# Small full-precision products packed into single passes, and the setup spread over the first steps, in a four-block convolution and attention kernel

## The chip, the cores and the metric

The kernel runs on one core of a Trainium2 chip. The metric is the device time of one execution in microseconds, the median of several. A core has the engines TensorE (PE, with its weight loads as PEld), VectorE (DVE), ScalarE (ACT), GpSimd (POOL) and SyncE (SP), which issues most DMAs. Each runs its own list of instructions in order and waits on semaphores for the others.

## What is computed

The input `x` is 32 images of 256 channels by 28 x 28 positions. Four blocks follow one another, each `x = x + block(gn(x))`, where `gn` is a group norm over 32 groups. Shortened, with the weights' names cut:

```python
# block 0: gated mix of 8 experts, one 256x256 matrix per image
g = sparsemax(gn_x.mean(axis=(2, 3)) @ gate_w.T + gate_b)
out = einsum('boi,bihw->bohw', einsum('bk,koi->boi', g, expert_w), gn_x)
# block 1: 3x3 depthwise, batch norm, relu, prune, 1x1, batch norm, relu, prune
h = prune(relu(bn(depthwise(gn_x, dw_w) + dw_b)), 4.0)
out = prune(relu(bn(conv1x1(h, pw_w) + pw_b)), 0.001)
# block 2: attention over the 784 positions as tokens
q, k, v = split(xt @ Wqkv + bqkv); q -= mean(q, axis=2); k -= mean(k, axis=2)
k2n = k*k / (sum(k*k, axis=2) + 1e-7);   q2n = q*q / (sum(q*q, axis=2) + 1e-7)
k2n /= max(norm(k2n, axis=-2), 1e-12);   q2n /= max(norm(q2n, axis=-1), 1e-12)
out = (v + q2n @ (k2n^T v) / sqrt(784)) @ Wln + bln
# block 3: 3x3 box mean
out = depthwise(gn_x, ones/9)
```

## The kernel before, in words

Channels lie on the 128 partitions, in two halves (`J` = 2). The images go through a pipeline of seven stages called Z, A, B, C_, D, E and F (`STAGES`): in step t, stage Z works on image t+1, A on t, B on t-1, and so on to F on t-5. Z loads an image and takes its sums; A is block 0; B is the depthwise part and C_ the 1x1 part of block 1; D makes queries, keys and their sums; E makes the attention output; F is the box mean. Every engine has one `step(t)` that writes its part of all stages in a fixed order, and `run` calls it for t = -1 to 36 (`run`, lines 345 to 355). The order of the work is thus the order of the lines in the five `step` functions, at 644 (TensorE), 982 (VectorE), 1273 (ScalarE), 1395 (GpSimd) and 394 (SP); semaphores carry the rest. Each step holds one product that gives the group means of all stages at once (`group_means`, 455), from which VectorE makes scale and shift (`variances`, `scales_shifts`, into `gn_avg`, `gn_rs`).

Precision: large products split each operand into a high part that fits the type `F32R` and the rest as a low part, and add three products (`by_parts`, 491). A few small products are in full fp32 instead. Three are touched here. `key_norms` (517) sums the squares of the keys per channel from `k_rows`, whose 128 rows hold 32 equal rows for each of four strips. `attention_weights` (525) adds the product of the keys' sums with the bias of the values, `bv_ln`, from the same rows. `query_scales` (587) spreads `q_alpha`, again 32 equal rows for each of four strips, over all partitions with one row of the identity as weights.

Results go on like this: ScalarE copies the keys' sums from PSUM (`key_rows`, 1148) and takes the root (`key_norms`, 1155); VectorE takes the reciprocal (931, 933); ScalarE and VectorE write the high and low parts `attn_parts` (1166, 935); TensorE's `attention_out` (543) waits for them. For the queries VectorE makes `q_alpha` (959), TensorE spreads it, VectorE multiplies (`scale_q`, 969).

Setup is two functions of the first step, t = 0 (`t.first`). TensorE's `setup` (420) multiplies the value and output matrices and makes biases. VectorE's `setup_weights` (701) waits for all loads, centres the query and key weights and their bias, makes the batch norm's scales and splits three weight matrices into parts; it stands ahead of `mixed_low`, on which the first convolution waits. In steps in which D has no image yet, the last five depthwise taps stand ahead of `make_x1` (1027); later they stand behind `scale_q` (1033). SP issues all loads first: x of image 0, the gate's, the other weights, the experts, then x of image 1.

## Time and profile before

| what | value |
|---|---|
| three timed runs | 1595.02, 1595.16, 1597.77 us; median 1595.16 |
| the profiled execution | 1597.63 us, its span 1596.0 us |
| TensorE busy | 1459.9 us (91%), VectorE 1361.9 (85%), ScalarE 1284.2 (80%), GpSimd 337.1 (21%) |
| mean granted clock of TensorE | 0.968 of full |
| steps 4 to 31 | 45.4 us each |
| start of step 4 (its `gn_avg`) | 158.18 us |

Busy times of the engines overlap, so their shares don't add up; the time goes by which engine the others wait for. Mean durations of operations that a step holds, from the list of groups by line (two halves of an image are two instructions; back to back, they overlap by some 0.1 us):

| engine, operation, line | mean us | | engine, operation, line | mean us |
|---|---|---|---|---|
| ACT `xn` 1072 | 1.035 | | DVE `hq_parts` 925 (`q_low`) | 0.970 |
| ACT `h` 1192 (first ReLU) | 1.029 | | DVE `k_inv` 931, 933 | 0.165, 0.166 |
| ACT `attn_parts` 1170 | 0.456 | | DVE `attn_parts` 938 | 0.481 |
| ACT `xn_parts` 1178 | 0.842 | | DVE `xn_parts` 945 | 0.973 |
| ACT `x3pad` 1089 | 1.038 | | DVE `x` 886 (`make_x3`) | 1.032 |
| ACT `over` 1202 and its read | 0.950 + 0.189 | | DVE `h` 827 (one tap) | 1.050 |
| ACT `k_rows` 1153 | 0.590 | | DVE `q_alpha` 967 | 1.378 |

The sparsemax and its weights are twelve operations on VectorE of 0.15 to 0.29 us, 2.6 us in a row. The value product's twelve records of one half take 2.1 us of TensorE, the attention output's 24 take 4.2.

### The profile page before, as it was taken

What the parts mean: (1) busy time and instruction counts of PE and PEld (TensorE: products, weight loads), DVE (VectorE), ACT (ScalarE), POOL (GpSimd) and SP (SyncE); (2) the same over time, 40 slices, a digit from 0 to 9 for tenths busy, and PEclk for the clock granted to TensorE, in tenths of its full rate; (3) what the DMA queues carried; (4) which work ended last, traced back from release to release, by engine and by line L of the source; (5) the groups of instructions that cost most, each with busy time, mean ns of one, the idle gap of its engine ahead of it and who ended that gap; (6) DMA issues with size and microseconds to landing.
All of it is one profiled execution on the core that took longest, in us unless ns stands there. A gap on an engine that the chain in (4) does not pass through costs nothing. (4 is left out here: it accounts for less than half of the span.)

```text
span 1596.0 us, 28994 instructions
## 1 busy us (share of the span) xinstructions
PE 1459.9 (91%) x9794; PEld 1298.9 (81%) x9794; DVE 1361.9 (85%) x2453; ACT 1284.2 (80%) x2568; POOL 337.1 (21%) x232
## 2 busy tenths in 40 slices
PE   3439999999999999999999999999999999998983
PEld 2327888888888888889888888898888888988883
DVE  5678899989999898989998988999989899998436
ACT  2258888888889888888899888888998888877752
POOL 2321112221222122212221222222212222111000
PEclk8669999999999999999999999999999999999997
DMA  3010134434443444344433433444434334444431
GB/s 131 20 41 21 39 64 89 94 82 82 102 101 82 79 91 90 80 80 101 101 83 78 95 86 80 82 100 101 86 75 100 82 82 90 71 82 81 82 61 41
DMA packets 45576, 127.92 MB, mean 80 GB/s; under 512 B 3794, under 2 KB 4818, under 8 KB 45523
## 3 DMA queue, kind: packets, MB, share of 16 engines
q0 software_dynamic: 24480, 72.26, 27.8%
q1 hardware_dynamic: 20946, 54.98, 9.8%
q8 instruction: 30, 0.49, 0.1%
q14 instruction: 24, 0.19, 0.0%
q10 hardware_dynamic: 96, 0.00, 0.0%
HBM read 29.29 MB, written 97.94 MB: 80 GB/s over the span
## 5 line engine op out<-in xcount | busy, mean ns | idle before, releaser
L827 DVE SCALAR_TENSOR_TENSOR h<-xpad,dw_sb,h 128x784 f32<-128x784 f32 x512 | 503.1, 1050 | 0.0
L1369 POOL TENSOR_SCALAR xpad<-x,gn_rs 128x784 f32<-128x784 f32 x64 | 107.7, 1691 | 513.1 <-DVE x L886 498.1
L640 PE MATMUL tile_ps<-k,xT 112*128 112x256 f32 x896 | 200.8, 382 | 0.0
L1380 POOL TENSOR_TENSOR x_parts<-x,x_parts 128x784 fp32r<-128x784 f32 x64 | 117.1, 1849 | 358.9 <-ACT x_parts L1126 358.9
L640 PEld LDWEIGHTS tile_ps<-k,xT 112*128 112x128 f32 x896 | 171.2, 192 | 22.3
L566 PE MATMUL tile_ps<-wqk,xn_parts 128*112 128x256 f32 x1344 | 187.4, 294 | 0.0
L1066 ACT ACTIVATE junk<-x 128x784 bf16<-128x784 f32 x192 | 163.2, 857 | 24.3 <-DVE x L876 13.1
L1393 POOL DMA_DIRECT2D out<-row_sums x90 | 107.9, 1199 | 341.0 <-DMA out<-row_sums 215.4
L566 PEld LDWEIGHTS tile_ps<-wqk,xn_parts 128*112 128x112 f32 x1344 | 169.3, 175 | 0.1
L485 PE MATMUL conv_ps<-hq_parts,attn_parts 128*128 128x392 f32 x768 | 145.3, 344 | 23.4 <-DVE attn_parts L938 23.4
L485 PEld LDWEIGHTS conv_ps<-hq_parts,attn_parts 128*128 128x128 f32 x768 | 135.3, 188 | 33.1 <-DVE attn_parts L938 33.1
L627 PE MATMUL conv_ps<-x_parts,mixed_parts 128*128 128x392 f32 (+1 forms) x768 | 149.2, 351 | 11.9 <-DVE mixed_parts L866 11.8
L627 PEld LDWEIGHTS conv_ps<-x_parts,mixed_parts 128*128 128x128 f32 x768 | 139.7, 194 | 14.8 <-issue 14.8
L485 PE MATMUL conv_ps<-xn_parts,w_out 128*128 128x392 f32 x768 | 150.8, 345 | 0.0
L485 PE MATMUL conv_ps<-hq_parts,pw_parts 128*128 128x392 f32 x768 | 145.9, 345 | 0.0
L485 PE MATMUL conv_ps<-xn_parts,wqk 128*128 128x392 f32 x768 | 142.7, 341 | 0.0
L485 PEld LDWEIGHTS conv_ps<-hq_parts,pw_parts 128*128 128x128 f32 x768 | 136.2, 189 | 1.7 <-DVE hq_parts L840 1.7
L485 PEld LDWEIGHTS conv_ps<-xn_parts,wqk 128*128 128x128 f32 x768 | 135.7, 188 | 0.0
L485 PEld LDWEIGHTS conv_ps<-xn_parts,w_out 128*128 128x128 f32 x768 | 134.3, 188 | 0.0
L945 DVE TENSOR_TENSOR xn_parts<-xn,xn_parts 128x784 fp32r<-128x784 f32 x64 | 59.6, 973 | 52.1 <-ACT xn_parts L1178 52.1
L1239 ACT ACTIVATE k<-tile_ps 112x256 f32<-112x256 f32 x224 | 82.8, 385 | 7.6 <-PE tile_ps L566 7.6
L1145 ACT ACTIVATE xT<-tile_ps,k_rec 112x256 f32<-112x256 f32 x224 | 88.0, 484 | 0.3 <-PE tile_ps L499 0.3
(154 smaller groups left out, 2825.2 us busy)
## 6 DMA issues: line engine op xcount, KB each, us to landing
out<-row_sums POOLq DMA_DIRECT2D x90, 784.0 KB, 7.1
x<-x SPq DMA_DIRECT2D x32, 784.0 KB, 4.3
out<-x SPq DMA_DIRECT2D x30, 784.0 KB, 3.4
expert_sb<-expert_rows SPq DMA_DIRECT2D x8, 256.0 KB, 4.9
out<-x SPq DMA_DIRECT2D x4, 392.0 KB, 2.3
x<-w_qk SPq DMA_DIRECT2D x1, 512.0 KB
x<-w_vT SPq DMA_DIRECT2D x1, 256.0 KB
x<-w_ln SPq DMA_DIRECT2D x1, 256.0 KB
```

The lines of the kernel that those rows point to most:

```text
L485: mm = nc.tensor.matmul(conv_ps[:, 2 * j + a, 0:HALF], wt[:, half(j)], act[:, a * HALF:(a + 1) * HALF], start=(first and i == 0), stop=(la ...
L566: mm = nc.tensor.matmul(dst, xn2_parts[:, u, i, m * TOK:(m + 1) * TOK], wqk[:, v, i, C:2 * C], start=False, stop=(i == J - 1 and u == 1))
L627: mm = nc.tensor.matmul(conv_ps[:, 2 * j + a, 0:width], mixed_parts[:, u, i * C + j * P:i * C + (j + 1) * P], x0_parts[:, v, i, a * HALF:a ...
L640: mm = nc.tensor.matmul(tile_ps[:, KX_BANK, i * C:(i + 1) * C], xT[:, m, half(i)], k2[:, m, :], start=(m == 0), stop=(m == M - 1))
L827: nc.vector.scalar_tensor_tensor(acc, view, scalar, acc, ALU.mult, ALU.add).then_inc(dw_step[j].sem, 1)
L945: nc.vector.tensor_tensor(xn2_parts[:, 1, j, :], xn2[:, j, :], xn2_parts[:, 0, j, :].bitcast(F32), ALU.subtract).then_inc(xn2_lo.sem, 1)
L1066: nc.scalar.activation(junk[:, j * HW:(j + 1) * HW], source[:, j, :], ACT.Square, accum_out=gn_in[:, layer, 2 + j:3 + j]).then_inc(gn_sums ...
L1145: nc.scalar.activation(xT[:, m, :], tile_ps[0:TOK, XT_BANK[m // 2], m % 2 * C:(m % 2 + 1) * C], ACT.Identity, scale=k_rec[:, m:m + 1]).the ...
L1239: nc.scalar.activation(k2[:, m, :], tile_ps[0:TOK, K_BANK[m // 2], m % 2 * C:(m % 2 + 1) * C], ACT.Square, accum_out=k_sum[:, m:m + 1]).th ...
L1369: nc.gpsimd.tensor_scalar(xpad[:, j, 1:1 + H, 1:1 + W], x1[:, B.odd, j, :].rearrange("p (h w) -> p h w", w=W), gn_r[:, 1, j:j + 1], gn_s[: ...
L1380: nc.gpsimd.tensor_tensor(x0_parts[:, 1, j, 0:HW], x0[:, Z.odd, j, :], x0_parts[:, 0, j, 0:HW].bitcast(F32), ALU.subtract).then_inc(x0_lo. ...
L1393: pool.dma_start(out_dram[F.times(1)], rows, accum_op=ALU.add).then_inc(rows_added[n].of(F), 16)
```

## The change

The three small products are packed. Of the 32 equal rows of a strip, some hold the high part of a value and the others its low part, and the weights on the other side divide by the number of rows that hold each part. One pass in `F32R` then adds what full precision took two records for. To make the rows, ScalarE's copy of the keys' sums becomes a multiplication with a column of ones and zeros (`low_row`) that rounds (`k_cut`), and VectorE gets a new subtraction, `key_rows`; two operations more make `alpha_cut` and `alpha_rows`. The masks come as further columns of `mix_const`.

The orders of `step` change: TensorE does the attention weights ahead of the gate's product; VectorE splits `q_low` round `key_norms`, does `attention_weights_low` ahead of `sparsemax` and both `make_x3` ahead of `h_mask`; ScalarE does `normalise_x2` ahead of `key_norms`, the attention highs between the two `relu_h`, and `x2_high` ahead of `normalise_x3`. The last five taps stand behind `make_x1` and `scale_q` in every step.

The setup is taken apart. The bias and the batch norm's variances (`setup_early`) stand ahead of VectorE's first step, the scales and the query and key weights (`setup_scales`, `setup_queries_keys`) in step 0, the rest (`setup_weights`) at the end of step 1. TensorE's `setup` moves to step 1. SP issues the query and key weights ahead of the experts, then x of image 1, then the other weights. ScalarE runs one small activation before anything else, and GpSimd's three short memsets come ahead of the long ones.

```diff
-        k_rows = sb("k_rows", [P, 2, C])
+        k_rows = sb("k_rows", [P, 2 * C], F32R)
+        k_cut = attn_parts[:, 0].rearrange("p j c -> p (j c)")
+        alpha_cut, alpha_rows = kx_parts[:, 0, 0, 0:QUARTER], kx_parts[:, 1, 0, 0:QUARTER]
...
-            for dst, src in loads:
-                sp.dma_start(dst, src).then_inc(w_loaded, 16)
+            for dst, src in early_loads:
+                sp.dma_start(dst, src).then_inc(early_loaded, 16)
+            sp.dma_start(wqk_raw, w_qk.rearrange("(j p) o -> p j o", p=P)).then_inc(wqk_loaded, 16)
             for g in range(PACKED):
                 for s in range(STRIPS):
                     sp.dma_start(expert_sb[:, g, s, :], expert_rows[:, g, s, :]).then_inc(experts_loaded, 16)
+            sp.dma_start(x0[:, 1], x_dram[1]).then_inc(x_loaded.sems[1], 16)
+            for dst, src in loads:
+                sp.dma_start(dst, src).then_inc(w_loaded, 16)
...
-                    mm = nc.tensor.matmul(tile_ps[:, KSUM_BANK, c:c + 1], k_rows[:, 1, half(c)], ones[:, 0:1], start=True,
-                                          stop=True, skip_group_check=True)
+                    mm = nc.tensor.matmul(tile_ps[:, KSUM_BANK, 2 * c:2 * c + 2], k_rows[:, C + c * P:C + (c + 1) * P],
+                                          norm_weight[:], start=True, stop=True, skip_group_check=True)
...
                     dst = tile_ps[:, ATTN_BANK, c * C:(c + 1) * C]
-                    nc.tensor.matmul(dst, k_rows[:, 0, half(c)], bv_ln[:], start=True, stop=False)
                     for i in range(J):
                         for u, v in ((0, 0), (0, 1), (1, 0)):
-                            mm = nc.tensor.matmul(dst, kx_parts[:, u, i, half(c)], w_out[:, v, i, :], start=False,
-                                                  stop=(i == J - 1 and u == 1))
+                            nc.tensor.matmul(dst, kx_parts[:, u, i, half(c)], w_out[:, v, i, :],
+                                             start=(i == 0 and u == v), stop=False)
+                    mm = nc.tensor.matmul(dst, k_rows[:, half(c)], bv_ln[:], start=False, stop=True)
...
                         mm = nc.tensor.matmul(tile_ps[:, ALPHA_BANK[a], s * QUARTER:(s + 1) * QUARTER],
-                                              idn[:, row:row + 1].to_broadcast([P, P]), q_alpha[:, 1, :], start=True,
+                                              picks[:, strip:strip + 1].to_broadcast([P, P]), alpha_rows, start=True,
                                               stop=True)
...
+                if t.number == 2:
+                    setup_done()
                 if E.active:
                     value_out(B, D, E, F, 0)
                     key_norms(E)
+                    attention_weights(E)
                 if A.active:
                     gate_logits(A)
                 if E.active:
-                    attention_weights(E)
                     value_out(B, D, E, F, 1)
-                if t.first:
+                if t.number == 1:
...
+            def setup_early():
+                dve.wait_ge(early_loaded, EARLY_LOADED)
+                for s in range(2):
...
+            def setup_scales():
+                dve.wait_ge(setup_act, 2)
+                for n, (bn, bias) in enumerate(((bn1_sb, dwb_sb), (bn2_sb, pwb_sb))):
...
+            def setup_queries_keys():
+                dve.wait_ge(wqk_loaded, 16)
                 for j in range(J):
...
+                parts_of(wqk, wqk_raw)
+
+            def setup_weights():
+                dve.wait_ge(w_loaded, LOADED)
...
-                did(nc.vector.tensor_scalar(bv_ln[:], tile_ps[:, 2, 0:C], 1.0 / SUB, None, ALU.mult))
+                cut = k_cut[:, 0:C]
+                did(nc.vector.tensor_scalar(cut, tile_ps[:, 2, 0:C], bias_low_row, None, ALU.mult))
+                did(nc.vector.tensor_tensor(bv_ln[:], tile_ps[:, 2, 0:C], cut.bitcast(F32), ALU.subtract))
+                did(nc.vector.tensor_scalar(bv_ln[:], bv_ln[:].bitcast(F32), bias_weight, None, ALU.mult))
+                did(nc.vector.tensor_copy(norm_weight[:], norm_row.to_broadcast([P, 2])))
+                did(nc.vector.tensor_copy(picks[:], pick_rows))
                 assert setup[0] == SETUP_DVE
+
+            setup_early()
...
+                nc.vector.tensor_tensor(k_rows[:], tile_ps[:, KSUM_BANK, :], k_cut.bitcast(F32),
+                                        ALU.subtract).then_inc(krow_ready.sem, 1)
...
+                nc.vector.tensor_scalar(alpha_cut, q_alpha[:, 1, :], low_row, None, ALU.mult).then_inc(alpha_step.sem, 1)
+                dve.wait_ge(alpha_step.sem, alpha_step.at(D, 3))
+                nc.vector.tensor_tensor(alpha_rows, q_alpha[:, 1, :], alpha_cut.bitcast(F32),
+                                        ALU.subtract).then_inc(alpha_step.sem, 1)
...
+                if E.active:
+                    key_rows(E)
...
                 if E.active:
-                    q_low(E)
+                    q_low(E, 0)
                     key_norms(E)
+                    q_low(E, 1)
+                    attention_weights_low(E)
                 if A.active:
                     sparsemax(A)
                     mean_lows(A)
-                if E.active:
-                    attention_weights_low(E)
-                if t.first:
-                    setup_weights()
+                if t.number == 0:
+                    setup_scales()
+                    setup_queries_keys()
                 if D.active:
                     x2_low(D)
                 if E.active:
                     make_x3(E, 0)
+                    make_x3(E, 1)
                 if C_.active:
                     h_mask(C_)
-                if E.active:
-                    make_x3(E, 1)
...
-                if B.active and not D.active:
-                    depthwise(B, slice(11, None))
                 if A.active:
                     make_x1(A)
                 if D.active:
                     scale_q(D)
-                if B.active and D.active:
+                if B.active:
                     depthwise(B, slice(11, None))
                 if D.active:
                     kx_low(D)
+                if t.number == 1:
+                    setup_weights()
...
-            act.wait_ge(setup_pool, SETUP_POOL)
+            act.wait_ge(setup_pool, SETUP_SMALL)
+            nc.scalar.activation(warm[:], zeros[:], ACT.Square).then_inc(setup_act, 1)
...
-                nc.scalar.copy(k_rows[:], tile_ps[:, KSUM_BANK, :].rearrange("p (a c) -> p a c", a=2)).then_inc(ksum_read.sem, 1)
+                nc.scalar.activation(k_cut, tile_ps[:, KSUM_BANK, :], ACT.Identity, scale=low_row).then_inc(ksum_read.sem, 1)
...
+                if D.active:
+                    normalise_x2(A, D)
                 if E.active:
                     key_norms(E)
-                if D.active:
-                    normalise_x2(A, D)
                 if C_.active:
                     relu_h(C_, 0)
-                    relu_h(C_, 1)
                 if E.active:
                     attention_weights_high(E)
+                if C_.active:
+                    relu_h(C_, 1)
+                if D.active:
+                    x2_high(D)
                 if F.active:
                     normalise_x3(F)
-                if D.active:
-                    x2_high(D)
```


The order of VectorE in a step in which all stages are at work, from the group norm's scales on. `gn_rs` are scale and shift, `box_rs` those of the box mean, `pooled` and `gate_in` the gate's input, `hq_parts` the queries' low parts, `z` and `zz` the beginning of the sparsemax. Before:

```order
L759 SCALAR_TENSOR_TENSOR gn_rs<-gn_avg,gn_rs 128x8
L767 TENSOR_SCALAR box_rs<-gn_rs 128x4
L773 SCALAR_TENSOR_TENSOR pooled<-gn_in,gn_rs 128x2
L776 TENSOR_TENSOR pooled<-pooled,gn_rs 128x2
L778 TENSOR_TENSOR gate_in<-gate_w_sb,pooled 128x16
L925 TENSOR_TENSOR hq_parts<-q2,hq_parts 128x784 x2
L931 TENSOR_SCALAR k_inv<-k_norm 128x2
L933 RECIPROCAL k_inv<-k_inv 128x2
L786 TENSOR_TENSOR z<-small_ps,gate_b_sb 128x8
L788 TENSOR_TENSOR zz<-z 128x64
```

After:

```order
L794 SCALAR_TENSOR_TENSOR gn_rs<-gn_avg,gn_rs 128x8
L967 TENSOR_TENSOR k_rows<-tile_ps,attn_parts 128x512
L802 TENSOR_SCALAR box_rs<-gn_rs 128x4
L808 SCALAR_TENSOR_TENSOR pooled<-gn_in,gn_rs 128x2
L811 TENSOR_TENSOR pooled<-pooled,gn_rs 128x2
L813 TENSOR_TENSOR gate_in<-gate_w_sb,pooled 128x16
L959 TENSOR_TENSOR hq_parts<-q2,hq_parts 128x784
L973 TENSOR_SCALAR k_inv<-k_norm 128x2
L975 RECIPROCAL k_inv<-k_inv 128x2
L959 TENSOR_TENSOR hq_parts<-q2,hq_parts 128x784
L980 SCALAR_TENSOR_TENSOR attn_parts<-tile_ps,k_inv,attn_parts 128x256 x2
L821 TENSOR_TENSOR z<-small_ps,gate_b_sb 128x8
```

A subtraction of 512 columns stands right behind the scales; the attention lows, which stood behind the whole sparsemax, now stand ahead of it.

ScalarE in the same stretch, from the keys' root on (`xn2` is the normalised image of stage D, `h` the ReLU of stage C_). Before:

```order
L1158 ACTIVATE k_norm<-tile_ps 128x2
L1072 ACTIVATE xn2<-x2,gn_rs 128x784 x2
L1192 ACTIVATE h<-h,bn_shift,bn_scale 128x784 x2
L1170 ACTIVATE attn_parts<-tile_ps,k_inv 128x256 x2
L1089 ACTIVATE x3pad<-x3,box_rs 128x28x28 x2
L1178 CAST xn2_parts<-xn2 128x784 x2
L1202 ACTIVATE over,h_over<-h,below 128x784 x2
```

After:

```order
L1126 ACTIVATE xn2<-x2,gn_rs 128x784 x2
L1213 ACTIVATE k_norm<-tile_ps 128x2
L1247 ACTIVATE h<-h,bn_shift,bn_scale 128x784
L1225 ACTIVATE attn_parts<-tile_ps,k_inv 128x256 x2
L1247 ACTIVATE h<-h,bn_shift,bn_scale 128x784
L1233 CAST xn2_parts<-xn2 128x784 x2
L1143 ACTIVATE x3pad<-x3,box_rs 128x28x28 x2
L1257 ACTIVATE over,h_over<-h,below 128x784 x2
```

The root stands behind `xn2`, the attention highs between the halves of `h`, and `xn2_parts` ahead of `x3pad`.

VectorE from the convolution of step 1 to the group means of step 2 (`h` are taps, `x1` the output of block 0). Before:

```order
L866 SCALAR_TENSOR_TENSOR mixed_parts<-small_ps,gn_rs,mixed_parts 128x256 x2
L827 SCALAR_TENSOR_TENSOR h<-xpad,dw_sb,h 128x784 x16
L876 SCALAR_TENSOR_TENSOR x1,gn_in<-conv_ps,x0 128x784 x2
L745 COPY gn_avg<-small_ps 128x16
L749 TENSOR_TENSOR gn_sq<-gn_avg 128x8
```

After, without the last three operations of the setup ahead of `gn_avg`:

```order
L901 SCALAR_TENSOR_TENSOR mixed_parts<-small_ps,gn_rs,mixed_parts 128x256 x2
L862 SCALAR_TENSOR_TENSOR h<-xpad,dw_sb,h 128x784 x11
L911 SCALAR_TENSOR_TENSOR x1,gn_in<-conv_ps,x0 128x784 x2
L862 SCALAR_TENSOR_TENSOR h<-xpad,dw_sb,h 128x784 x5
L715 CAST pw_parts<-x3 128x512
L716 TENSOR_TENSOR pw_parts<-x3,pw_parts 128x512
L715 CAST w_out<-tile_ps 128x512
L716 TENSOR_TENSOR w_out<-tile_ps,w_out 128x512
L765 TENSOR_TENSOR b_out<-tile_ps,params 128x2
L766 COPY bq_col<-tile_ps 128x2
L768 TENSOR_SCALAR attn_parts<-tile_ps,mix_const 128x256
L769 TENSOR_TENSOR bv_ln<-tile_ps,attn_parts 128x256
```

Eleven taps stand ahead of `x1` and five behind it, and then the last part of the setup.

## Rows read from the trace of the kernel before

A timeline row gives start, duration, engine, line, operation, operands and count, and in brackets the idle time before it and what ended it.

**Rows 1.** Windows, ten steady steps: us, busy time and count per engine, clock, DMA share

```profile
656.90:1110.90 454.00, 446.24 (x3038) 399.08 (x3034) 413.05 (x740) 398.86 (x799) 105.02 (x70) 1.00 0.42 88
```

**Rows 2.** Waits of TensorE and VectorE, same ten steps: total, times, longest

```profile
PE conv_ps L485 <- DVE attn_parts L938: 7.8, 10, 0.8
...
DVE xn_parts L945 <- ACT xn_parts L1178: 17.3, 10, 1.7
...
DVE attn_parts L938 <- ACT attn_parts L1170: 6.6, 10, 0.7
...
DVE ymask L848 <- ACT over L1221: 4.2, 10, 0.5
```

**Rows 3.** Timeline of weight loads, one step: start, us, instruction and count

```profile
705.45 0.59 PEld L521 LDWEIGHTS tile_ps<-ones,k_rows 128*128 128x128 f32 x4
...
705.96 0.53 PEld L476 LDWEIGHTS small_ps<-gate_in,ones 128*128 128x128 f32 x4
...
706.41 0.30 PEld L531 LDWEIGHTS tile_ps<-bv_ln,k_rows 128*128 128x128 f32 x2
...
708.68 2.10 PEld L485 LDWEIGHTS conv_ps<-xn_parts,w_out 128*128 128x128 f32 x12
...
721.57 0.76 PEld L566 LDWEIGHTS tile_ps<-wqk,xn_parts 128*112 128x112 f32 x6
...
739.19 1.36 PEld L594 LDWEIGHTS tile_ps<-q_alpha,idn 128*128 128x128 f32 x8
```

**Rows 4.** Timeline of VectorE, the same step

```profile
703.16 0.68 DVE L979 TENSOR_TENSOR kx_parts<-tile_ps,kx_parts 128x512 fp32r<-128x512 f32 x1
...
704.83 0.17 DVE L759 SCALAR_TENSOR_TENSOR gn_rs<-gn_avg,gn_rs 128x8 f32<-128x8 f32 x1
...
735.50 0.26 DVE L962 TENSOR_SCALAR q_alpha<-q_norm 128x196 f32<-128x196 f32 x1
```

**Rows 5.** Timeline of ScalarE, the same step

```profile
716.70 1.79 ACT L1211 ACTIVATE hq_parts<-h,hmask 128x784 fp32r<-128x784 f32 x2 [0.24 <-DVE hmask L834]
...
735.07 0.31 ACT L1264 ACTIVATE q_norm<-tile_ps 128x196 f32<-128x196 f32 x1
```

**Rows 6.** Waits of ScalarE, the ten steps of rows 1

```profile
ACT q L1248 <- PE conv_ps L485: 4.9, 10, 0.5
...
ACT h L1186 <- issue: 2.4, 10, 0.3
```

**Rows 7.** Timeline of VectorE, start of the program

```profile
11.38 1.50 DVE L751 SCALAR_TENSOR_TENSOR gn_var<-gn_avg,gn_sq 128x8 f32<-128x8 f32 x1
...
17.81 0.16 DVE L858 TENSOR_TENSOR x_parts<-gn_avg,x_parts 128x4 fp32r<-128x4 f32 x1
...
37.99 0.88 DVE L866 SCALAR_TENSOR_TENSOR mixed_parts<-small_ps,gn_rs,mixed_parts 128x256 fp32r<-128x256 f32 x2
...
81.35 0.17 DVE L745 COPY gn_avg<-small_ps 128x16 f32<-128x16 f32 x1 [1.75 <-PE small_ps L469]
...
117.30 0.18 DVE L745 COPY gn_avg<-small_ps 128x16 f32<-128x16 f32 x1 [1.96 <-PE small_ps L469]
```

**Rows 8.** Windows, sums: setup's query-key and scale parts; then its `pw_parts`, `w_out` parts

```profile
sum 7.99, PE 2.44 PEld 2.18 DVE 7.16 ACT 0.94 POOL 0.00; mean PE 0.81 PEld 0.73 DVE 2.39 ACT 0.31 POOL 0.00
...
sum 3.49, PE 0.00 PEld 0.00 DVE 3.25 ACT 0.85 POOL 0.00; mean PE 0.00 PEld 0.00 DVE 1.62 ACT 0.43 POOL 0.00
```

**Rows 9.** Windows, 20 to 25 us

```profile
20.00:25.00 5.00, 1.40 (x7) 1.30 (x7) 4.55 (x14) 0.00 (x0) 0.00 (x0) 1.00 0.00 0
```

**Rows 10.** Windows, TensorE's setup

```profile
15.15:27.04 11.89, 8.29 (x29) 6.64 (x33) 10.53 (x38) 0.00 (x0) 0.00 (x0) 1.00 0.19 71
```

**Rows 11.** Timeline of TensorE, alpha products of the last steps

```profile
1464.00 2.02 PE L594 MATMUL tile_ps<-q_alpha,idn 128*128 128x196 f32 x8 [2.20 <-DVE q_alpha L967]
...
1506.96 1.59 PE L594 MATMUL tile_ps<-q_alpha,idn 128*128 128x196 f32 x8 [1.91 <-DVE q_alpha L967]
...
1545.95 2.98 PE L594 MATMUL tile_ps<-q_alpha,idn 128*128 128x196 f32 x8 [1.54 <-DVE q_alpha L967]
```

More of the change, by code:

```diff
@@ L32 @@
 UNROLL = 2
+HIGH_ROWS, BIAS_LOW_ROWS = SUB // 2, SUB // 4
+PATTERNS = 4 + STRIPS
 STAGES = 7
@@ L83, in first, with number @@
     @property
-    def first(self):
-        return self.pair is None and self.offset == 0
+    def number(self):
+        return self.offset if self.pair is None else None
     @property
@@ L369, in build @@
         ]
-        loads = [
+        early_loads = [
             (params[:], channel_params),
             (bqk_row, b_qk[None, :]),
-            (wqk_raw, w_qk.rearrange("(j p) o -> p j o", p=P)),
+        ]
+        loads = [
             (wvT_sb, w_vT.rearrange("(j p) o -> p j o", p=P)),
@@ L920, in box_row_sums, with q_low, key_rows @@
                 nc.vector.tensor_tensor(*row_operands(1), ALU.add).then_inc(row_step.sem, 1)
-            def q_low(E):
-                for j in range(J):
-                    dve.wait_ge(q_hi.sem, q_hi.at(E, j + 1))
-                    nc.vector.tensor_tensor(q_parts[:, 1, j, :], q2[:, j, :], q_parts[:, 0, j, :].bitcast(F32),
-                                            ALU.subtract).then_inc(q_lo.sem, 1)
+            def q_low(E, j):
+                dve.wait_ge(q_hi.sem, q_hi.at(E, j + 1))
+                nc.vector.tensor_tensor(q_parts[:, 1, j, :], q2[:, j, :], q_parts[:, 0, j, :].bitcast(F32),
+                                        ALU.subtract).then_inc(q_lo.sem, 1)
+            def key_rows(E):
+                dve.wait_ge(ksum_read.sem, ksum_read.at(E))
+                if (E - 1).active:
+                    dve.wait_ge(attn_w_mm.sem, attn_w_mm.at(E - 1))
+                nc.vector.tensor_tensor(k_rows[:], tile_ps[:, KSUM_BANK, :], k_cut.bitcast(F32),
+                                        ALU.subtract).then_inc(krow_ready.sem, 1)
             def key_norms(E):
@@ L1302, in step @@
                         first_tap(B, j)
-                if t.first:
-                    setup()
+                if t.number == 0:
+                    setup_bias()
                 for m in range(M):
@@ L1329, in step @@
                     x0_high(Z)
-                if t.first:
-                    act.wait_ge(setup_dve, SETUP_DVE)
+                if t.number == -1:
+                    setup_root()
                 if C_.active:
@@ L1429 @@
     group_mean = ((c[:, None] // GROUP) == (c[None, :] // GROUP)).astype(np.float32) / (GROUP * HW)
+    row, strip = c % SUB, c // SUB
+    low, bias_low = row >= SUB - BIAS_LOW_ROWS, (row >= HIGH_ROWS) & (row < SUB - BIAS_LOW_ROWS)
+    picked = (strip[:, None] == np.arange(STRIPS)[None, :]) & ((row == 0) | (row == SUB - 1))[:, None]
     per_channel = {
```

108 lines of the change are left out of this document (62 added, 46 removed).

## The prediction

> **What bounds the kernel now.** I read the table of slices first (TensorE nearly full from 120 us on), then the busy time of a steady stretch, then who waits there, then one step instruction by instruction. Ten steps take 454.0 us, so a step is 45.4 us; TensorE is busy 446.2 us of them, VectorE 413.1, ScalarE 398.9 [rows 1]. TensorE looks like the bound, but it waits once per step, 7.8 us in ten, for `attn_parts`, the low halves that VectorE makes [rows 2]. VectorE waits in three places only: 17.3 us for `xn_parts`, 6.6 for `attn_parts`, 4.2 for `ymask` [rows 2]. That is 28.1 us; take it from 454.0 and VectorE is tied up 425.9 us, 42.6 us a step: 41.3 of work and the rest the small gaps between instructions. TensorE is tied up 44.6 (45.4 less 0.78). So both engines run almost without slack, and what one gets back the other must be able to follow. Below, every position in a step counts from the end of `gn_rs` (704.83 + 0.17 = 705.0 us), called zero.
>
> **TensorE: what goes.** Starts of weight loads give the pace. The two `k_norm` products (four records) hold TensorE from 705.45 to 705.96, 0.51 us. The attention weights hold it from 706.41 to 708.68, 2.27 us, for 16 records. The alpha products hold it for 1.36 us, eight records [rows 3]. A full-precision product stands as two records; a packed one as one, and six of those on 256 columns have their weights loaded in 0.76 us, 0.127 each [rows 3]. Afterwards: two records, 0.25; 14 records, 1.78; four records, 0.51. Saved: 0.26 + 0.49 + 0.85 = 1.60 us a step. No row shows a packed product on 196 or 2 columns, so the bounds are the 0.127 of the 256-column row and today's 0.17 a record, two records a product (1.36 for the four, nothing saved on alpha). I take the first, as the nearest row of the same kind; the other costs nothing where VectorE is the bound, since TensorE then still needs only 44.6 - 0.75 = 43.9. TensorE's need becomes 44.6 - 1.6 = 43.0 us.
>
> **VectorE: what comes.** Per step a 512-wide subtraction with one operand in PSUM (0.68 us, as `kx_parts`) and two 196-wide operations (0.26 us, as the `q_alpha` row) [rows 4]; with some 0.04 us of gap each and a per-partition scalar in one of them I take 1.35 us. Bounds: 1.2 without gaps, 1.7 if the two short ones cost as much as half a 392-wide one and wait for each other. ScalarE's copy of the sums becomes a scaled write of the same 512 columns, no longer.
>
> **What the new order does.** On ScalarE `x2_high` goes ahead of `normalise_x3` (two halves, some 1.9 us), on VectorE the attention lows go ahead of the gate's twelve small operations, and `q_low` is split round `key_norms`. Followed from zero, with the durations of the table above the rows: VectorE writes `k_rows` by 0.72, the gate inputs by 1.4, `q_low` 2.4, `k_inv` 2.75, second `q_low` 3.7. TensorE starts the norms at 0.8, ends the weights about 2.9, the gate product 3.35, second value product 5.5. ScalarE: `xn2` to 2.0, norms 2.2, first ReLU 3.2, attention highs 4.0. VectorE waits 0.35 us, ends the lows at 4.95, before TensorE wants them at 5.5: the 0.78 us wait of TensorE goes. The gate ends at 7.55, and ScalarE has had `xn_parts` ready since 7.2: the 1.73 us wait goes too. Both `x3` are done at 11.3, the mask at 11.6, where ScalarE's sums (11.35) come late for the first time. From there ScalarE is solid: mask to `q_norm` was 716.70 to 735.07, 18.4 us [rows 5], of which 0.49 (q) and 0.24 (h) were waits for TensorE and GpSimd [rows 6] that are earlier now; 17.65 us remain, so `q_norm` stands ready at 29.6. VectorE gets there at 29.45. It then adds the two alpha operations (0.6 with gaps), which swallow the 0.38 us wait at `ymask` [rows 4].
>
> **Sum of a step.** 42.6 + 1.35 = 43.95 us of VectorE, and waits of 0.35 (attention highs), about 0.2 (`q_norm`) and 0.1 elsewhere: 44.6 us. The chain walked above closes at 44.75. I take 44.6, a gain of 0.8 us over 45.4, in the 28 steps in which every stage but the last is at work (4 to 31): 22 us. TensorE then idles 1.6 us a step, mostly before the norm products: VectorE is the bound. Half of the 1.6 us saved is not seen.
>
> **Start.** Ahead of the first convolution VectorE sits in setup from 17.97 (17.81 + 0.16) to 37.99 [rows 7]; afterwards only the scales and the query-key part stand there, 7.99 us [rows 8], and with the start 0.7 later (below) `mixed_low` starts near 26.7 instead of 38.0, 11.3 earlier. The 0.7 is the centring of the bias, some 5 us that now stand ahead of the first `gn_avg` and overrun it by 1 to 2 us, partly paid by ScalarE's table load, warmed up early. All loads have landed before 20 us [rows 9], so the new order of SP's queue (experts before x of image 1, weights last) delays nobody: who waits on `w_loaded` needs it after 40 us. SP waits for nothing there. The eleven are given back in step 1. TensorE's own setup, 15.15 to 27.04 with 8.3 us of work in it [rows 10], now stands ahead of `mix_experts`, whose weights VectorE has ready 2.9 us after the gate product: 8.3 - 2.9 = 5.4 us lost. `setup_weights` then sits on VectorE ahead of the next `gn_avg`: its old parts take 3.5 us [rows 8], and four new small operations 1.4, together 4.9 us. In the other direction the last five taps now come behind `make_x1`, so that they cover the 1.75 and 1.96 us that VectorE waits for the group means in steps 1 and 2 [rows 7]. Step 2 starts 11.3 - 5.4 + 1.7 - 4.9 = 2.7 us earlier, step 3 another 1.9: 4.6, of which I take 4 (1 to 9).
> `gn_var`, on eight columns, takes 1.50 us [rows 7] while GpSimd runs its two subtractions; the centring now falls into that stretch. The Trainium skill (SBUF — State Buffer, section SBUF: two separate sides) says that a VectorE operation with two SBUF inputs and a GpSimd operation hold a shared port in turn; this agrees with the row, and by it each of the two bias subtractions could lose up to one GpSimd operation.
>
> **End.** In the last steps TensorE's wait for `attn_parts` and its products are on the path, and so are the new alpha operations. Steps 32 and 33 give about 1 each (their waits for `q_alpha`, 2.20 and 1.91 us [rows 11], grow to 3), 34 gives 1.3, 35 gives 0.7: 4 us.
>
> **Total.** 22 + 4 + 4 = 30 us. The profiled execution took 1597.6 us with a span of 1596.0; it lies at the top of the three timed runs, whose median is 1595.2. So 1567.6 for an execution like the profiled one, and from the median, which the forecast is for, 1565 us.
>
> **Rivals.**
> A, VectorE follows further: its waits all vanish and its additions cost 1.2; the step is 43.8, 1.6 less, 45 us in 28 steps, with start and end 53: about 1545 us, or 1552 where TensorE or ScalarE holds back a little. For it speaks that every wait of VectorE is under 2 us; against it that ScalarE and VectorE are level at two places.
> B, the steady steps gain almost nothing: the additions cost 1.7, `q_norm` or the attention highs come 0.4 later than walked; step 45.3, and only start and end pay: 1586 us. That the packed products are not shorter at 196 and 2 columns leads to nearly the same (TensorE's need is 44 and its start now hangs on `k_rows`): also about 1586.
> C, slower: the clock. TensorE's new wait ahead of the norm products is near 1.5 us. After a wait of 2.20 us the alpha products took 2.02 us, after one of 1.91 they took 1.59; after 1.54 behind a longer one, 2.98 [rows 11]. So it is not one wait alone that counts. If the wait reaches about 2 us and the clock falls there, the weights (1.8 us) take twice that; the attention highs, and VectorE behind them, come 2 us later; step 46.6. In every step this is 1.2 x 28 = 34 us lost less the 8 of start and end: 1621 us; in every second step 1604. It decides at a wait of 2 us. Against it: the granted clock is 1.00 in the whole steady stretch [rows 1] with a wait of 0.78.
> The Trainium skill (TensorE: Matmul & The Clock Gate, section on HAM oscillation) warns that repeated idle gaps let the array fall back to half its clock; rows 11 agree for single gaps, and by this rule the time would be that of C.
>
> **How the numbers follow.** Forecast (1557 to 1574 by itself) 0.50, A 0.18, B 0.24, C 0.08. The range leaves out C and the ends of A and B: 1546 to 1590. What a measurement of this kernel can tell from no change is 0.2%, 3.2 us. Faster by more: the forecast, A and most of B, 0.88; within: 0.04; slower: 0.08.
>
> **What would show it.** Right: steady steps of 44.6 us; VectorE with one wait of 0.3 to 0.4 us for the attention highs and none for `xn_parts`; TensorE waiting 1 to 2 us for `k_rows` and no longer for `attn_parts`; alpha products in 0.5 us; starts of steps 2 and 3 near 79 and 113 us. Wrong: alpha products that still take 1.3 us, a clock under 1.00 in the steady stretch, `gn_avg` waiting for TensorE (TensorE still bound), or an `x1` of step 1 that no longer waits on the setup.

## The result and the profile after

The changed kernel takes 1546.7 us (median of 4 runs, 1546.2 to 1547.1), the kernel before 1595.4 beside it: ratio 0.969, 95% interval 0.967 to 0.970. I had said 1565. It is faster by 48.7 us where 30 were forecast, and lies at the lower end of my range.

Where the 50.3 us between the two profiled executions are, by the starts of `gn_avg` (the first instruction of a step on VectorE): by step 4 the changed kernel is 5.1 us ahead (158.18 against 153.09), by step 32 46.3, by the last 50.3. So the start gave 5.1 us (forecast 4), the 28 full steps 41.2 (forecast 22), the end 4.0 (forecast 4). A full step takes 44.00 us on average in place of 45.47: 1.47 saved, where I took 0.8. Of the three terms only that one is far off.

Ten steps of the changed kernel, columns as in [rows 1]:

```profile
681.20:1121.30 440.10, 429.53 (x2972) 383.02 (x2971) 420.94 (x771) 396.92 (x800) 97.20 (x70) 1.00 0.43 91
```

The waits in these ten steps, as in [rows 2] and [rows 6]:

```profile
ACT gn_sd L1114 <- DVE gn_var L786: 14.0, 10, 1.5
...
PE tile_ps L540 <- DVE k_rows L967: 10.6, 10, 1.1
ACT kx_parts L1325 <- PE tile_ps L659: 10.4, 10, 1.1
...
DVE attn_parts L980 <- ACT attn_parts L1225: 4.1, 10, 0.4
...
DVE hmask L869 <- ACT over L1257: 2.3, 10, 0.3
```

VectorE's waits for `xn_parts` and `ymask` are gone, TensorE's for `attn_parts` too. TensorE now waits 1.06 us a step for `k_rows`, at full clock all the time (1.00 in the window's line). Its weight loads, as in [rows 3]:

```profile
727.27 0.30 PEld L540 LDWEIGHTS tile_ps<-norm_weight,k_rows 128*128 128x128 f32 x2 [1.41 <-DVE k_rows L967]
727.48 0.78 PEld L552 LDWEIGHTS tile_ps<-w_out,kx_parts 128*128 128x128 f32 x6
...
729.12 0.53 PEld L495 LDWEIGHTS small_ps<-gate_in,ones 128*128 128x128 f32 x4
...
759.00 0.59 PEld L613 LDWEIGHTS tile_ps<-kx_parts,picks 128*128 128x128 f32 x4
759.51 1.17 PEld L659 LDWEIGHTS tile_ps<-k,xT 112*128 112x128 f32 x6
```

From start to start: norms 0.21, weights 1.64 (14 records), alpha 0.51 (four). Packed products cost the 0.127 us a record that I had taken, or a little less, on 196 and 256 columns alike. By these starts 1.78 us are saved a step; by TensorE's busy time in full steps 1.50 (ten steps: 444.5 us with the new orders alone, below, against 429.5). And VectorE in the same step, as in [rows 4] and [rows 5]:

```profile
726.44 0.17 DVE L794 SCALAR_TENSOR_TENSOR gn_rs<-gn_avg,gn_rs 128x8 f32<-128x8 f32 x1
726.52 0.69 DVE L967 TENSOR_TENSOR k_rows<-tile_ps,attn_parts 128x512 fp32r<-128x512 f32 x1
727.13 0.16 DVE L802 TENSOR_SCALAR box_rs<-gn_rs 128x4 f32<-128x4 f32 x1
...
737.64 0.17 DVE L869 TENSOR_SCALAR hmask<-h_over 128x2 f32<-128x2 f32 x1 [0.18 <-ACT over L1257]
...
755.53 0.26 DVE L1004 TENSOR_SCALAR q_alpha<-q_norm 128x196 f32<-128x196 f32 x1
755.83 1.38 DVE L1009 RECIPROCAL q_alpha<-q_alpha 128x196 f32<-128x196 f32 x1
757.25 0.32 DVE L1013 TENSOR_SCALAR kx_parts<-q_alpha,mix_const 128x196 fp32r<-128x196 f32 x1
757.60 0.36 DVE L1015 TENSOR_TENSOR kx_parts<-q_alpha,kx_parts 128x196 fp32r<-128x196 f32 x1
757.88 0.16 DVE L883 TENSOR_SCALAR ymask<-y_over 128x2 f32<-128x2 f32 x1
...
763.89 4.81 DVE L862 SCALAR_TENSOR_TENSOR h<-xpad,dw_sb,h 128x784 f32<-128x784 f32 x5
```

The last row, the last five depthwise taps, is the place that I had not priced. The same five in the kernel before:

```profile
743.56 5.15 DVE L827 SCALAR_TENSOR_TENSOR h<-xpad,dw_sb,h 128x784 f32<-128x784 f32 x5
```

GpSimd of the kernel before at the same time:

```profile
740.70 3.39 POOL L1380 TENSOR_TENSOR x_parts<-x,x_parts 128x784 fp32r<-128x784 f32 x2 [8.90 <-ACT x_parts L1126]
```

and GpSimd of the changed kernel:

```profile
760.57 3.38 POOL L1440 TENSOR_TENSOR x_parts<-x,x_parts 128x784 fp32r<-128x784 f32 x2 [8.88 <-ACT x_parts L1180]
```

Before, the five taps began at 743.56 while GpSimd was busy until 744.09, and took 5.15 us. Now GpSimd ends at 763.95, as they begin, and they take 4.81.

Counted from `gn_avg` (at 749.23 before, 725.36 after), the row sums start at 13.80 and 12.49, `q_alpha` at 31.65 and 30.17, and the step ends at 45.53 and 43.86: most of the gain, 1.31 us, is made ahead of the row sums. The changed kernel mostly alternates between steps of 43.86 and 44.18. Half of that difference, 0.17 us, is there before the row sums start; the other half lies in them: in every second step the second `xpad` operation runs first and the first row sum is held for 0.7 us (2.47 in place of 1.79), in the others that `xpad` operation is held (3.60 us for the two in place of 1.98), and after it the second row sum (2.31).

### The profile page after: what moved, and what is told of

It is laid out like the page before. It is cut to its first block and busy times, and to the rows that moved or that the text cites. A ratio compares the mean times of both kernels' runs of the same rounds, so it can differ in the third digit from the quotient of the medians.

```text
span 1545.4 us, 28737 instructions
## 1 busy us (share of the span) xinstructions
PE 1404.6 (91%) x9538; PEld 1246.2 (81%) x9538; DVE 1389.4 (90%) x2553; ACT 1277.0 (83%) x2569; POOL 312.1 (20%) x232
## 5 line engine op out<-in xcount | busy, mean ns | idle before, releaser
L862 DVE SCALAR_TENSOR_TENSOR h<-xpad,dw_sb,h 128x784 f32<-128x784 f32 x512 | 493.6, 1031 | 0.0
L659 PE MATMUL tile_ps<-k,xT 112*128 112x256 f32 x896 | 204.7, 387 | 0.0
L1429 POOL TENSOR_SCALAR xpad<-x,gn_rs 128x784 f32<-128x784 f32 x64 | 87.5, 1373 | 483.3 <-DVE x L921 461.4
L1440 POOL TENSOR_TENSOR x_parts<-x,x_parts 128x784 fp32r<-128x784 f32 x64 | 112.3, 1772 | 339.3 <-ACT x_parts L1180 339.3
L631 PE MATMUL small_ps<-expert_sb,mix_w 128*32 128x512 f32 x512 | 66.7, 641 | 8.2 <-DVE mix_w L851 8.2
```

Source lines behind the costliest of these rows:

```text
L631: mm = nc.tensor.matmul(small_ps[s * SUB:(s + 1) * SUB, :], mix_w[:, g, :], expert_sb[:, g, s, :], start=(g == 0), stop=(g == PACKED - 1), ...
L659: mm = nc.tensor.matmul(tile_ps[:, KX_BANK, i * C:(i + 1) * C], xT[:, m, half(i)], k2[:, m, :], start=(m == 0), stop=(m == M - 1))
L862: nc.vector.scalar_tensor_tensor(acc, view, scalar, acc, ALU.mult, ALU.add).then_inc(dw_step[j].sem, 1)
L1429: nc.gpsimd.tensor_scalar(xpad[:, j, 1:1 + H, 1:1 + W], x1[:, B.odd, j, :].rearrange("p (h w) -> p h w", w=W), gn_r[:, 1, j:j + 1], gn_s[: ...
L1440: nc.gpsimd.tensor_tensor(x0_parts[:, 1, j, 0:HW], x0[:, Z.odd, j, :], x0_parts[:, 0, j, 0:HW].bitcast(F32), ALU.subtract).then_inc(x0_lo. ...
```

## Experiments

All ratios are to runs of the kernel before on the same chip, whose medians lay between 1595.4 and 1600.1 us. That kernel itself varies between 1595 and 1601 us from one execution to the next, so differences of a few us are better read from the steps of the profiles than from the medians. "Step" is the mean over steps 4 to 31, from the starts of `gn_avg` in each profile.

| run | us | ratio (95%) | step |
|---|---|---|---|
| before | 1595.4 | 1 | 45.47 |
| a_packed_only | 1599.0 | 1.000 (0.999 to 1.001) | 45.44 |
| c_act_order_only | 1577.7 | 0.988 (0.985 to 0.991) | 44.76 |
| c_dve_order_only | 1606.7 | 1.006 (1.004 to 1.008) | 45.77 |
| a_orders_only | 1568.1 | 0.981 (0.979 to 0.984) | 44.44 |
| a_packed_and_orders | 1555.0 | 0.974 (0.972 to 0.976) | 44.03 |
| a_start_only | 1585.8 | 0.994 (0.992 to 0.996) | 45.44 |
| after | 1546.7 | 0.969 (0.967 to 0.970) | 44.00 |
| b_pe_extra | 1550.0 | 0.970 (0.968 to 0.972) | 44.06 |
| b_pool_shift | 1556.7 | 0.975 (0.972 to 0.977) | 44.31 |
| b_xpad_early | 1545.0 | 0.966 (0.964 to 0.969) | 43.94 |
| c_sums_late | 1545.9 | 0.967 (0.966 to 0.969) | 44.02 |
| c_xpad_and_sums | 1539.9 | 0.964 (0.962 to 0.966) | 43.74 |
| b_alpha_unpacked | 1538.7 | 0.962 (0.960 to 0.965) | 43.89 |
| d_alpha_and_xpad | 1541.3 | 0.965 (0.963 to 0.966) | 43.80 |
| d_before_pieces | 1596.2 | 1.000 (0.999 to 1.001) | 45.45 |

**Taking the change apart: products, orders, setup.** The edits are the hunks of the diff shown above, each group alone.

> The kernel before with the three products packed and VectorE's and ScalarE's work for it, in the old orders of the step, setup as before. Theory (VectorE binds; the packed products alone save TensorE time that nobody is waiting for): VectorE has 1.37 us more, of which the wait of 1.7 us for xn_parts takes a part; step 45.2 to 45.8, time 1590 to 1605. Rival (TensorE binds and its 1.6 us a step are the gain): step near 43.9, time 1550.

> The kernel before with the new orders of the steady step on TensorE, VectorE and ScalarE, and nothing packed, setup as before. Theory (VectorE and ScalarE set the step by their waits, which the orders take away): VectorE's waits of 2.8 us a step fall under 1 us, and the step then ends on TensorE, which needs 44.6: step 44.6 to 44.8, time about 1575 (1571 to 1580). Rival (the gain comes from TensorE's packed products, the orders bring nothing alone): 1590 to 1596.

> The changed kernel with the setup of the kernel before: products packed and the new orders, start as before. Theory (terms add): 1547 + 5 = 1552 us, steady steps 43.86 and 44.18 in turn. Rival (start and steady state hang together, for instance the parity in which GpSimd and VectorE meet is set in the start): steady steps of another length, time off 1552 by more than 3 us.

> The kernel before with the changed setup alone (the setup taken apart and spread over steps 0 to 2, the loads in the new order, the last five taps behind make_x1 in the first steps); steady steps, products and orders as before. In the changed kernel the start gave 5.1 us by the starts of gn_avg. Theory (the start is a term of its own): 1590 us, steady steps still 45.4. Rival (the setup saves the 11 us that it takes away ahead of the first convolution and does not give them back, the rest being the slower products): 1584 or less.

Packing alone brings nothing measurable: VectorE's wait for `xn_parts` is the same 1.73 us a step as in [rows 2], and what TensorE saves is idle time. VectorE's wait in ten steps:

```profile
DVE xn_parts L969 <- ACT xn_parts L1213: 17.3, 10, 1.7
```

The orders alone bring 1.03 us a step, and then TensorE is busy without a hole, 444.52 of 444.52 us. (VectorE's waits fall to 2.1 us a step, not under 1, since TensorE now holds the step; the time, 1568, is a little below the 1571 to 1580 that I expected.) Ten steps, columns as in [rows 1]:

```profile
691.41:1135.93 444.52, 444.52 (x3052) 400.16 (x3051) 411.04 (x741) 396.80 (x801) 89.29 (x70) 1.00 0.43 90
```

Only then is packing worth something: 0.41 (44.44 to 44.03) of 1.50 us, until other engines are level. The setup alone gave 8.9 us by step 4, against 5.1 in the changed kernel. Of the 3.8 us between them 1.3 are the new small operations at the end of step 1 (1.78 us from start to start where the setup alone has 0.46); where the rest goes is open. I had expected 5, with 11 as the rival; it lies between, and the parts of the start do not add exactly. The full steps do not depend on the start: a_packed_and_orders has steps of 43.84 and 44.18 in turn as well, 44.03 on average, and takes 1555 us where 1552 were expected.

One thing in a_packed_only bears on the clock. TensorE waits twice in most of its steps, on average 0.8 us for `k_rows` and 0.9 for `attn_parts`, and in six of the 28 full steps the granted clock is 0.96 in place of 1.00. One of the six, and the step behind it, columns as in [rows 1]:

```profile
614.27:659.95 45.68, 44.65 (x299) 39.92 (x298) 42.39 (x79) 40.03 (x80) 8.93 (x7) 0.96 0.42 88
659.95:705.31 45.36, 43.37 (x299) 38.32 (x298) 42.34 (x79) 40.10 (x80) 10.49 (x7) 1.00 0.42 89
```

TensorE is busy 1.3 us longer in such a step, but the step is only some 0.15 us longer than its neighbours of the same parity (45.64 against 45.50), since TensorE has idle time there.

**Which order.** The new order of ScalarE alone, then that of VectorE and TensorE alone:

```
 ScalarE step:  normalise_x2, norms, relu 0, attention highs, relu 1, x2_high, normalise_x3
 before:        norms, normalise_x2, relu 0, relu 1, attention highs, normalise_x3, x2_high
```

> The kernel before with ScalarE's new order alone (x2_high ahead of normalise_x3, norms behind normalise_x2, attention highs between the two ReLUs). Theory (VectorE's wait of 1.73 us for xn_parts is what the orders take away, and it is ScalarE's order that causes it): that wait goes, TensorE's wait for attn_parts stays, step 44.7 to 45.0, time 1576 to 1586. Rival (what counts is TensorE's wait of 0.78 us for attn_parts, which VectorE's order takes away): 1592 to 1597.

> The kernel before with the new orders of VectorE and TensorE alone (attention lows ahead of the gate, q_low split, both x3 ahead of the mask, weights ahead of the gate product). Theory of the first case: VectorE still waits 1.7 us for xn_parts, step 45.2 to 45.5, time 1588 to 1597. Rival (TensorE's wait counts): step 44.7, time 1576.

ScalarE's order alone makes a step of 44.76, of which TensorE is busy 44.70; the ten steps:

```profile
695.63:1143.53 447.90, 447.02 (x3052) 399.75 (x3051) 405.82 (x741) 396.94 (x801) 89.20 (x70) 1.00 0.42 90
```

VectorE's order alone costs 0.3 us a step, because it asks for the attention highs before ScalarE, still in its old order, has written them. Its waits, ten steps:

```profile
DVE attn_parts L937 <- ACT attn_parts L1168: 30.8, 10, 3.1
```

I had expected about no change, and it is slower: the two waits of the kernel before, 1.73 us for `xn_parts` and 0.66 for the attention highs, became one of 3.08.

**Is TensorE's slack real?**

```
+ pe.wait_ge(kx_lo.sem, kx_lo.at(E))
+ for n in range(8): matmul(tile_ps[:, ATTN_BANK, 0:C], kx_parts[:, 0, 0, half(0)], w_out[:, 0, 0, :], start=True, stop=True)
  pe.wait_ge(krow_ready.sem, krow_ready.at(E))
```

> The changed kernel (1547 us) with eight more packed records on 256 columns a step on TensorE, 1.0 us, put ahead of its wait for k_rows; they only repeat a product whose result is overwritten. Theory (VectorE binds, TensorE has 1.06 us of slack there): the wait falls to about 0.1 us and the time is 1547 to 1550. Rival (TensorE still binds, its saving is what the change gained): step longer by 1.0, 1547 + 28 = 1575.

28 us of extra work in the full steps cost about 3 (2 of them in the full steps). The wait for `k_rows` falls from 1.06 to 0.14 us a step (its weight load still waits 0.4). TensorE does not bind.

**The port.** One small GpSimd operation ahead of `x_parts`:

```
+ nc.gpsimd.tensor_tensor(spare, ones, ones, subtract)    # 128x224, 0.55 us
```

> The changed kernel (1547 us) with one more GpSimd operation of some 0.5 us (224 columns) ahead of its x_parts subtractions, so that these end about 0.5 us later and run into the start of VectorE's last five taps, as they did in the kernel before. Nobody waits for them at that point. Theory (the two engines hold the SBUF port in turn; in the changed kernel the taps start just as GpSimd is done): the five taps take 5.2 to 5.3 us in place of 4.81, step longer by 0.4, time 1547 + 11 = 1558 (1555 to 1562). Rival (the taps were slower in the kernel before for another reason, GpSimd is off the path): 1547, taps 4.81.

GpSimd in one step of it:

```profile
765.30 3.38 POOL L1443 TENSOR_TENSOR x_parts<-x,x_parts 128x784 fp32r<-128x784 f32 x2
```

and VectorE:

```profile
768.08 5.21 DVE L863 SCALAR_TENSOR_TENSOR h<-xpad,dw_sb,h 128x784 f32<-128x784 f32 x5
```

GpSimd now ends at 768.68, 0.6 after the taps' start, and they take 5.21 us again; the time is up by 9 to 10 us, the step by 0.31. Nobody waits for GpSimd here, so this is the two engines' meeting alone. In the kernel before I tried the reverse, with the subtractions cut into four:

```
+ for n in range(4): cols = slice(n * HW // 4, (n + 1) * HW // 4); ... x0_parts[:, 1, j, cols] ...
```

> The kernel before with GpSimd's x_parts subtractions cut into four pieces each (196 columns), nothing else changed: the collision with the last five taps is taken away in the kernel before itself. Theory (a VectorE operation waits until the running GpSimd operation ends, so short ones cost it little): the last taps take 4.8 to 4.9 us in place of 5.1 to 5.2, and since VectorE and TensorE are both nearly full, the step falls by 0.1 to 0.35: 45.1 to 45.4, time 1586 to 1594. Rival (the taps' length in the kernel before has nothing to do with GpSimd): taps 5.15, time 1596.

This failed as a cure. The eight pieces take 5.73 us in place of 3.39 and meet three taps of 1.3 us each in place of one of 1.4; the mean of all taps rises from 1051 to 1077 ns. Groups of VectorE's operations, ten steps (busy us, mean ns, idle before):

```profile
L827 DVE SCALAR_TENSOR_TENSOR h<-xpad,dw_sb,h 128x784 f32<-128x784 f32 x162 | 163.8, 1077 | 0.0
...
L938 DVE SCALAR_TENSOR_TENSOR attn_parts<-tile_ps,k_inv,attn_parts 128x256 fp32r<-128x256 f32 x20 | 8.8, 480 | 2.3 <-ACT attn_parts L1170 2.3
```

But it tells something else: 0.4 us more on VectorE changed no time, since its wait for `attn_parts` shrank from 6.6 to 2.3 us in ten steps. In the kernel before such a delay is paid out of a wait; in the changed one it is on the path. In a_packed_only and in c_act_order_only the taps take 155.2 and 154.5 us in ten steps in place of 157.5: there the collision had mostly ended by the timing alone. In the kernel before, with its own timing and without the collision, no run was made.

**Who holds the step now?** Three reliefs, alone and together.

```
 xpad_early:     pool.wait_ge(xn2_lo.sem, xn2_lo.at(E + 1))       (was: x3_ready.at(E, 1))
 sums_late:      ScalarE: key squares first; sum_squares(3, ...) behind x0_high, i.e. behind q_norm
 alpha_unpacked: idn and q_alpha in full precision again; the two 196-wide VectorE operations out
```

> The changed kernel (1547 us) with one wait of GpSimd changed: its two xpad operations start once VectorE has written xn_parts, about 1 us earlier, so that they run beside the two x3 operations (one operand in PSUM) and not beside the row sums (both in SBUF). Theory (the port is held in turn): xpad takes 1.99 us for two in every step, the row sums 1.79 each in place of 4.05 to 4.27 for both, VectorE has 0.5 to 0.65 us less a step; TensorE needs 42.95, so the step falls from 44.0 to 43.4, time 1530 (1527 to 1536). Rival (the row sums are hidden, or another wait takes the place): 1545 to 1548.

> The changed kernel (1547 us) with ScalarE's stretch between the mask and q_norm shorter: the key squares first and the sums of squares of x3 (1.7 us) moved behind q_norm, where ScalarE waits over 1 us for TensorE. Theory (VectorE and ScalarE reach q_norm together, 30.2 us after gn_avg; to relieve one alone brings nothing): 1543 to 1548. Rival (ScalarE alone sets q_norm): step 43.4, time 1530.

> The two reliefs together: GpSimd's xpad started earlier, off the row sums (0.5 to 0.7 us a step less on VectorE, alone worth 2 us or nothing in time), and ScalarE's sums behind q_norm. Theory (both engines had to be relieved): q_norm is read 29.7 us after gn_avg in place of 30.2 to 30.5, every step 43.3 to 43.5, time 1528 to 1533. Rival (something else holds the step at 43.9, TensorE or a transfer): 1543 to 1547.

Starting `xpad` early does what it should: both row sums take 1.79 us in every step. It hardly shows in the time, 0.06 us a step. In the shorter of the two kinds of step `q_alpha` starts 30.17 us after `gn_avg` in both kernels: VectorE now arrives early and waits for ScalarE, 0.27 us at `k_eps` and 0.1 at `q_norm`. Its waits, without the last one, which is too short for the list:

```profile
DVE attn_parts L980 <- ACT attn_parts L1225: 4.2, 10, 0.4
DVE gn_rs L792 <- ACT gn_sd L1114: 2.7, 10, 0.3
DVE k_eps L993 <- ACT k L1294: 2.7, 10, 0.3
```

ScalarE's relief alone is worth nothing either; ScalarE then waits for TensorE's query product, in c_sums_late and with both reliefs alike:

```profile
ACT q L1303 <- PE conv_ps L504: 11.4, 10, 1.2
```

Both together give 0.26 us a step, less than the 0.5 to 0.7 that I expected. (The start also loses 2.3 us by step 4.) Up to `q_norm` the expectation held: averaged over steps 5 to 31, `q_alpha` starts 29.86 us after `gn_avg` in place of 30.33, 0.47 earlier. The loss comes behind it: the last five taps, now early, meet GpSimd again, and from the second of them on only 0.27 is left. So 0.20 of the shortfall is the port once more. GpSimd and VectorE in one step:

```profile
759.31 3.39 POOL L1441 TENSOR_TENSOR x_parts<-x,x_parts 128x784 fp32r<-128x784 f32 x2 [9.50 <-ACT x_parts L1180]
```

```profile
762.27 5.05 DVE L862 SCALAR_TENSOR_TENSOR h<-xpad,dw_sb,h 128x784 f32<-128x784 f32 x5
```

> The changed kernel (1547 us) with the alpha products in full precision again (eight records, +0.85 us on TensorE) and without VectorE's two 196-wide operations (0.75 us with gaps). Theory (VectorE binds, TensorE has 1.06 us of slack): VectorE needs 43.3, TensorE 43.8, so the step is 43.8 to 43.9, time 1541 to 1546. Rival (packing alpha is part of the gain, TensorE's 0.85 us comes back): 1547 + 24 = 1571.

Ten steps of it:

```profile
676.83:1116.66 439.83, 438.48 (x3012) 391.80 (x3011) 416.56 (x751) 397.06 (x801) 94.02 (x70) 1.00 0.44 91
```

The packing of alpha, by itself, costs: without it the medians differ by 8 us, the profiled spans by 4.9 (3.0 in the full steps, 1.9 ahead of step 4). With c_xpad_and_sums, from which its time cannot be told, it is the best version found, ahead of both kernels. TensorE, busy 438.5 of 439.8 us, is then the bound (three of its 28 steps take 44.8 us, the others 43.8), and the early `xpad` adds nothing to it:

> The changed kernel with alpha unpacked (1539 us by itself) and xpad started earlier (1545 by itself). Theory (with alpha unpacked TensorE never waits and holds the step at 43.8; relief of VectorE brings no more): 1536 to 1540. Rival (the reliefs add): 1532 to 1535, step 43.6.

Ten steps:

```profile
679.04:1117.14 438.10, 438.07 (x3012) 391.88 (x3011) 411.43 (x751) 396.97 (x801) 89.11 (x70) 1.00 0.44 92
```

TensorE is busy 438.07 of 438.10 us; the time, 1541.3, is a little above what I expected and cannot be told from that without the early `xpad`.

## Why the prediction came out low on the gain

**TensorE: right.** Norms, weights and alpha save 0.30, 0.63 and 0.85 by the starts of their loads, where I had 0.26, 0.49 and 0.85 [rows 3]; the place of the new wait and its size (1.06; I had said 1 to 2) held, and b_pe_extra shows that it is slack. "Half of the 1.6 us saved is not seen" was too kind: with the orders in place, 0.41 of the 1.50 shows.

**The step that failed: "42.6 + 1.35 = 43.95 us of VectorE".** The waits that I added to it, 0.65, are right in sum: 0.41 for the attention highs and 0.23 at the mask, and none that the list of waits shows at `q_norm`, where I had 0.2. So VectorE is tied up 44.00 - 0.64 = 43.36 us, 0.59 less than that sum. The 42.6 was itself 0.1 too small: the window of [rows 1] is 454.0 us long, while the ten steps there, from the `gn_avg` at 658.23 to that at 1113.23, take 455.0. So the step before was 45.5, VectorE was tied up 42.7 us of it, and the change added 0.67 us to that, not 1.35. (A fourth wait of VectorE, 0.27 us for `gn_sd`, is in both figures.) Three pieces of the difference are known:
- 42.6 was carried over from before as if work had a fixed length. It holds 0.37 us (157.5 against 153.8 us in ten steps for the taps) of collision with GpSimd, which the new timing happened to end. That was luck: nothing in the change aimed at it, and my sum did not have it. b_pool_shift puts it back and gets 0.31 us a step, 9 to 10 us in all.
- The row sums lose a little less to `xpad` too, 0.08 us a step (42.6 against 41.9 us in ten steps).
- The 1.35 priced each added operation by its duration and a gap. `k_rows` lasts 0.69 us but takes 0.61 from its start to the next one's, and it fills the gap between `gn_rs` and `box_rs`: from the one's start to the other's took 0.25 us on average before and takes 0.74 with `k_rows` between them. The insertion costs 0.49, where I had 0.72. The alpha operations cost 0.63 from start to start, as I had taken (0.6). My walk had the attention lows done at 4.95 from zero; they were at 4.63.

That the first piece is on the path of the changed kernel is shown; the other two are read from rows and have no run of their own. By size the three, 0.37, 0.08 and 0.23, cover the 0.68 between 1.35 and 0.67.

**"VectorE is the bound": half right.** From `q_norm` to the next mask it is. Between the mask and `q_norm` VectorE and ScalarE are level: b_xpad_early and c_sums_late, each relieving one, gave 2 us or less by their medians, both together 7. I had seen ScalarE as solid there, and 17.65 us for it; it took 17.33 from the mask (737.85) to `q_norm` (755.18).

**The kernel before.** I took ScalarE's late `xn_parts` as one of three waits; it was the lead one. c_act_order_only moves three calls on one engine and gives 0.71 of the 1.47 us. After it TensorE is all but full, and my figure of 44.6 for its need is 44.45 where it is full (a_orders_only).

**Start: right in its sum, not in its parts.** The first `gn_avg` comes 3.4 us later, not 0.7:

```profile
8.37 1.94 DVE L730 CAST xT<-xn 1x512 bf16<-1x512 f32 x1
10.35 1.94 DVE L731 TENSOR_TENSOR xn<-xn,xT 1x512 f32<-1x512 f32 x1
12.32 0.41 DVE L732 CAST xT<-xn 1x512 bf16<-1x512 f32 x1
12.77 0.68 DVE L733 TENSOR_TENSOR xn<-xn,xT 1x512 f32<-1x512 f32 x1
```

The same copy and the same subtraction took 1.94 us while GpSimd's `x_parts` ran (8.17 to 11.74) and 0.41 and 0.68 after it. That is 2.8 us lost; without it the first `gn_avg` would have come 0.7 later, as I took. I had named this risk beside [rows 7] and not put it into the sum. The Trainium skill (SBUF — State Buffer, section SBUF: two separate sides) names, besides operations with two SBUF inputs, those in a 2-port mode, which a copy from SBUF to SBUF can enter; the trace agrees, since the copy with its one input lost no less than the subtraction (1.94 us in place of 0.41). `mixed_low` starts at 28.06, 9.9 us earlier in place of 11.3; steps 2 and 3 start at 77.0 and 111.1, forecast 79 and 113, so less was given back in step 1 than I took. The start is right by errors that cancel.

**End: right** (4.0 us). The alpha products wait 2.66, 2.66 and 2.31 us there [rows 11], where I had said 3.

**Rivals.** The time is that of rival A (1545 or 1552), but for other reasons: VectorE's waits did not all vanish, its work became shorter. (From the median its sum, 53 us, gives 1542, not 1545.) B fell: the additions cost less, not more. C fell for this kernel: the granted clock is 1.00 with 1.06 us of wait in each step. But what it fears is real: a_packed_only, with two waits of 0.8 and 0.9 us in a step, lost the full clock in six of 28 steps. The Trainium skill (TensorE: Matmul & The Clock Gate, section on HAM oscillation) tells of repeated gaps, in its example longer ones than here; the changed kernel's single gap of 1.06 us a step did not lead there.

## What to carry over

An engine's occupied time is not a sum of fixed lengths: subtract what it loses to collisions, and ask whether the new timing keeps them. Price an added instruction from start to start, and take off what it fills of a gap between two dependent ones. With three engines over 90% full, look for the one order whose output is late before saving work; a saving counts only up to the next engine, and giving back a saving that costs the new bound (alpha) can be faster. After each relief look at the collisions again: a shift of 0.4 us brought one back.

## What the runs showed of the hardware

- A VectorE operation that meets a GpSimd one on SBUF is held until about its end, and the other way round: two `xpad` operations take 1.98 us alone and 3.60 with a row sum beside them; a five-tap group 4.81 alone and 5.05 to 5.22 where its first tap meets the end of `x_parts`. It also holds for a plain copy of one SBUF operand (0.41 against 1.94 us), while operations with an operand in PSUM beside the same GpSimd work kept their length (`x<-conv_ps,x` 1.04).
- Cutting a GpSimd operation into four raised the collisions, as eight pieces took 5.73 us in place of 3.39 and held three taps in place of one.
- TensorE's granted clock stayed at 1.00 in the full steps with one wait of 1.06 us in each (changed kernel) or one of 0.78 (before), and was 0.96 in six of 28 steps with two waits, 0.8 and 0.9 us (a_packed_only).
